# Attention plus int8 feed-forward on eight cores: value groups and projections in other slots, the last value product of the odd pairs one step earlier, one copy for a value group

## The chip, the cores and the metric

The kernel runs on all 8 NeuronCores of one Trainium2 chip, four cores to a die. Every core works on its own four sequences of the input and the cores exchange nothing. The metric is the device time of the slowest core in microseconds (us). Three runs of the kernel before gave 1652.48, 1654.83 and 1738.67 us, median 1654.83. The engines are called as in the profile: PE (matrix products), DVE (vector), ACT (scalar), POOL (GpSimd) and SP (the engine that issues most DMAs).

## The reference

The input is x, 32 sequences of 2048 rows of 1024 numbers. Rows are normalised, and two branches work on the result:

```python
xn = _layernorm(x, axis=-1)
x = x + _L0_attn_ref(xn, w_in, w_out) + _L0_ffn_ref(xn, weight_q, weight_scale, bias)
```

The attention has 16 heads of 64 and works in windows of 512 queries. Each window sees its own 512 keys and the 512 before it, of which the mask keeps those at a distance of 0 to 512; a bias that grows with the distance is added before the softmax. The first window of a sequence has no keys before it.

```python
scores = jnp.einsum('bhnqd,bhnkd->bhnqk', qb, k2) * scale
scores = jnp.where(valid, scores + bias, -jnp.inf)
p = jax.nn.softmax(scores, axis=-1)
out = jnp.einsum('bhnqk,bhnkd->bhnqd', p, v2)      # then times w_out
```

The feed-forward branch is a quantised linear layer: each row is scaled to at most 127 and rounded, multiplied by an int8 weight of 1024 by 1024, and scaled back.

## The kernel before, in words

A core holds 16 **blocks** of 512 rows, four to a sequence. The program is recorded by a Python loop (`for t ... for slot ... for i ...`, lines 856 to 957) which appends instructions to one list for each engine; every engine then executes its list strictly in that order and waits only on semaphores. A block has 8 **slots** (one for each pair of heads) and a slot has 5 **steps**. The text numbers the steps of a block from 0 to 39: step = 5 x slot + i.

In each step of a block the loop records these things, in this order.

- `scores` (slots 0 to 2) or `scores2` (slots 3 to 7) for one tile of 128 keys by 512 queries of a head pair. In slots 0 to 2 each step does its own. From slot 3 on, the even steps do the scores of two steps at once ("paired scores": steps 22 and 23 in step 22, steps 24 and 25 in step 24), into the two score buffers `sc0` and `sc1`, which alternate by step.
- `exps2` of an odd step in slots 3 to 7: ACT turns the scores into exponentials in `p`.
- the evacuations of the product group of the step before (list `after`), by ACT or DVE.
- `norm` if one is due: DVE multiplies the sums in `oa` and `ob` by the reciprocals and writes `ofm` (lines 845 and 848).
- `mask` of the step before: DVE multiplies `p` by a triangle (line 806).
- `den` if one is due: ACT makes the reciprocals of the row sums as Ln, Ln and Exp(-x) (lines 835, 837, 838). It waits for the last value product of its pair.
- `exps`, or `exps2` of an even step.
- one **dense group** from the table `PLAN`: 8 matmuls of 512 columns into one of two PSUM buffers `dn0`, `dn1`, used in turn. K and Q are the key and query projections, V the value projection of this block (`("V", half, chunk)`), F the int8 product and P the output projection of the block before (`("F", chunk, half)`). A `+` marks the next block. A third group can start only when the first one's buffer has been evacuated. V groups are evacuated by ACT (two copies, lines 627 and 628), F by DVE (line 649), P by DVE (line 681), after which POOL adds the residual (line 664) and SP stores the result; K and Q groups of pairs 3 to 7 by DVE (line 599), of pairs 0 to 2 by ACT and DVE.
- `pv`: the value products (line 822) of exponentials of earlier steps, by the table in braces at line 891: the tile of a slot's step i is multiplied at step i + 4, 4, 5, 5 and 6 counted from the tile's slot start for i = 0, 1, 2, 3, 4 (the first two 4 steps after the start, the next two 5, the last one 6).
- the preparation of the next block (statistics, normalisation) and of the rounded input of the block before (`xq_make`, three POOL operations for each half of a row tile; `xq_turn`, a DMA transpose on SP's queue), by tables of steps.

`den` stands 7 steps after its slot's start and `norm` one after it. For the pair of slot 3 (start 15) that is steps 22 and 23, for slot 4 (start 20) steps 27 and 28, for slot 5 (start 25) steps 32 and 33.

## Time and profile before

| what | value |
|---|---|
| runs | 1652.48, 1654.83, 1738.67 us |
| the profiled execution's own time | 1654.68 us |
| its span on the slowest core | 1653.1 us |
| spans of all cores | 1645.1 to 1653.1 us |
| granted clock, mean of each core | 0.992 to 0.994 |
| busy: PE, ACT, DVE, POOL | 95%, 64%, 57%, 51% |
| chain that ended last, by engine | PE 85%, ACT 6%, DMA 4% |

The profiled execution stands 0.15 us below the median of the runs. A matmul's row gives a start and a modelled duration; a matmul of 512 columns is listed with 0.38 us while the next one starts 0.22 us later, so the starts, not the durations, tell what PE spends. The time in square brackets behind a row is the idle time before it and what ended it.

### The profile page before, as it was taken

How to read it: one execution, taken by the hardware profiler on the slowest of the kernel's cores; microseconds unless marked ns; L12 is line 12 of the kernel's file. 1: busy time of each engine (PE TensorE's matmuls, PEld its weight loads, DVE VectorE, ACT ScalarE, POOL GpSimd, SP SyncE). 2: the span in 40 equal slices, each digit the busy share in tenths (PEclk: the TensorE clock that was granted, in tenths of full speed). 3: DMA queues.
4: the chain of work that ended last, by engine and by line, in shares of the span. 5: the costliest groups of instructions: out<-in, count | busy, mean ns of one | idle time of the engine just before them, and what ended most of it. 6: DMA issues, size and time to landing. Idle time of an engine off the chain costs nothing.

```text
span 1653.1 us, 29485 instructions; the slowest of 8 cores (1645.1 to 1653.1 us)
## 1 busy us (share of the span) xinstructions
PE 1566.1 (95%) x8568; PEld 749.9 (45%) x8736; DVE 939.6 (57%) x1696; ACT 1060.1 (64%) x2093; POOL 840.0 (51%) x1242
## 2 busy tenths in 40 slices
PE   4859999999999999999999999999999999999998
PEld 2325444454444445444444544445444444544443
DVE  4535646556475655746566564655647566564454
ACT  3546676766746667776665677667775566767662
POOL 5324536445473644536455563645537554563365
PEclk9979999999999999999999999999999999999999
DMA  7784453433545344353445434344354634435232
GB/s 161 185 222 116 124 147 107 128 116 122 147 133 151 115 128 121 113 146 114 128 132 149 142 109 136 113 121 135 109 141 127 173 116 115 141 109 147 78 79 82
DMA packets 208707, 213.98 MB, mean 129 GB/s; under 512 B 139932, under 2 KB 140060, under 8 KB 208040
## 3 DMA queue, kind: packets, MB, share of 16 engines
q1 hardware_dynamic: 205672, 201.60, 42.2%
q0 software_dynamic: 2880, 10.49, 3.5%
q8 instruction: 76, 1.25, 0.3%
q14 instruction: 79, 0.65, 0.2%
HBM read 149.12 MB, written 37.75 MB: 113 GB/s over the span
## 4 chain that ended last, share of the span: by engine, by line
PE 85%; ACT 6%; DMA 4%; issue 3%; DVE 1%; POOL 1%; SPq 0%; ACTq 0%; DVEq 0%; POOLq 0%
PE dn L578 61%; PE ob L822 7%; PE oa L822 7%; PE sc L730 5%; PE sc L753 5%; ACT p L770 4%; DMA wqk<-w 1%; DMA w2bf<-wqk 1%; ACT r L837 1%; ACT r L835 1%; DMA xpre<-x 1%; SPq L160 0%; DVE p L806 0%; POOL xn L462 0%; DMA xnfm<-xn 0%
## 5 line engine op out<-in xcount | busy, mean ns | idle before, releaser
L770 ACT ACTIVATE p<-sc,kbias_sb 128x512 bf16<-128x512 f32 (+3 forms) x1120 | 489.9, 536 | 235.8 <-PE sc L753 158.6
L578 PE MATMUL dn<-xnfm,wqk 128*128 128x512 bf16 x1996 | 477.1, 382 | 14.6 <-DMA xnfm<-xn 9.6
L664 POOL TENSOR_TENSOR u<-u,xres 128x256 f32<-128x256 f32 x240 | 169.9, 729 | 337.8 <-DVE u L681 337.5
L806 DVE TENSOR_TENSOR p<-p,tri_sb 128x512 bf16<-128x512 bf16 (+1 forms) x608 | 251.3, 414 | 146.4 <-ACT p L787 112.5
L578 PEld LDWEIGHTS dn<-xnfm,wqk 128*128 128x128 bf16 x2048 | 192.6, 98 | 244.5 <-issue 34.4
L787 ACT ACTIVATE p<-sc 128x1024 bf16<-128x1024 f32 (+3 forms) x228 | 214.9, 954 | 107.8 <-PE sc L730 105.9
L578 PE MATMUL dn<-wq_sb,xqfm 128*128 128x512 bf16 x1003 | 240.5, 381 | 6.0 <-DMA xqfm<-xq 2.8
L578 PE MATMUL dn<-wout_sb,ofm 128*128 128x512 bf16 x984 | 233.0, 379 | 6.5 <-issue 4.0
L578 PE MATMUL dn<-wv_sb,xnfm 128*128 128x512 bf16 x985 | 237.2, 380 | 2.0
L822 PE MATMUL oa<-p,vst 128*128 128x512 bf16 (+3 forms) x888 | 217.4, 300 | 4.6 <-DVE ofm L848 4.4
L822 PE MATMUL ob<-p,vst 128*128 128x256 bf16 (+3 forms) x896 | 218.7, 300 | 0.4
L649 DVE SCALAR_TENSOR_TENSOR u<-dn,small,wsb_sb 128x512 f32<-128x512 f32 x124 | 93.1, 751 | 166.9 <-PE dn L578 160.3
L681 DVE TENSOR_TENSOR u<-dn,u 128x512 f32<-128x512 f32 x124 | 85.8, 692 | 177.0 <-PE dn L578 165.3
L561 POOL TENSOR_TENSOR xres<-xres,biasb_sb 128x256 f32<-128x256 f32 x248 | 168.1, 709 | 0.0
L578 PEld LDWEIGHTS dn<-wv_sb,xnfm 128*128 128x128 bf16 x1024 | 97.6, 98 | 116.0 <-issue 10.7
L445 POOL TENSOR_SCALAR small<-small 128x1 f32<-128x1 f32 x64 | 12.3, 192 | 267.8 <-DVE small L444 267.8
L578 PEld LDWEIGHTS dn<-wq_sb,xqfm 128*128 128x128 bf16 x1024 | 96.6, 98 | 112.7 <-issue 13.8
L578 PEld LDWEIGHTS dn<-wout_sb,ofm 128*128 128x128 bf16 x1024 | 95.2, 98 | 114.2 <-issue 14.1
L753 PE MATMUL sc<-q,k 64*128 64x512 bf16 (+3 forms) x1120 | 117.4, 301 | 25.4 <-ACT p L770 22.4
L835 ACT ACTIVATE r<-oa 64x512 f32<-64x512 f32 x128 | 76.1, 594 | 87.8 <-PE ob L822 85.9
L822 PEld LDWEIGHTS oa<-p,vst 128*128 128x128 bf16 x896 | 87.9, 98 | 88.9 <-issue 8.3
L543 POOL TENSOR_SCALAR xqt<-xres,small 128x512 f32<-128x512 f32 x124 | 99.4, 802 | 40.3 <-DMA xres<-x 28.8
(61 smaller groups left out, 1634.4 us busy)
## 6 DMA issues: line engine op xcount, KB each, us to landing
wqk<-w2bf SPq DMA_DIRECT2D x240, 256.0 KB, 3.0
xpre<-x SPq DMA_DIRECT2D x64, 512.0 KB, 4.5
xres<-x SPq DMA_DIRECT2D x64, 512.0 KB, 4.5
out<-u SPq DMA_DIRECT2D x124, 256.0 KB, 2.2
wqk<-w POOLq DMA_DIRECT2D x16, 256.0 KB, 8.7
w2bf<-wqk SPq DMA_DIRECT2D x16, 256.0 KB, 5.5
wv_sb<-wv POOLq DMA_DIRECT2D x2, 1024.0 KB, 11.8
wq_sb<-wq POOLq DMA_DIRECT2D x1, 2048.0 KB, 13.8
```

The source lines that it names most:

```text
L543: a = P.op("gpsimd", lambda e, cols=cols: e.tensor_scalar(out=xqt[:, :], in0=buf[:, cols], scalar1=negm[g][:, tc:tc + 1], scalar2=alpha[g] ...
L561: xb_ready[(t, tc)] = P.op("gpsimd", lambda e, cols=cols: e.tensor_tensor(out=buf[:, cols], in0=buf[:, cols], in1=biasb_sb[:, cols], op=AL ...
L578: tok = P.op("tensor", lambda e, k=k: e.matmul(out=dn[b][:, :], lhsT=lhs(k), rhs=rhs(k), start=(k == 0), stop=(k == n - 1)), waits=(waits ...
L649: v = P.op("vector", lambda e: e.scalar_tensor_tensor(out=u[:, :], in0=dn[b][:, :], scalar=xs[g][:, tc:tc + 1], in1=wsb_sb[:, cols], op0=A ...
L664: a = P.op("gpsimd", lambda e, q=q: e.tensor_tensor(out=u[:, 256 * q:256 * q + 256], in0=u[:, 256 * q:256 * q + 256], in1=buf[:, 512 * hal ...
L681: v = P.op("vector", lambda e: e.tensor_tensor(out=u[:, :], in0=dn[b][:, :], in1=u[:, :], op=ALU.add), waits=[tok, u_ready[(t, tc, half)]])
L753: tok = P.op("tensor", lambda e, r=r, slot=slot, tc=tc, c0=c0, c1=c1, hp=hp: e.matmul(out=sc[b % 2][:, 512 * hp + c0:512 * hp + c1], lhsT= ...
L770: tok = P.op("scalar", lambda e, c0=c0, c1=c1, hp=hp, o=o: e.activation(out=pbuf[b % NPB][:, 512 * hp + c0:512 * hp + c1], in_=sc[b % 2][: ...
L787: exp_done[b] = P.op("scalar", lambda e: e.activation(out=pt, in_=st, func=AF.Exp, scale=SCALE), waits=[sc_done[b]] + p_free[b % NPB])
L806: mask_done[b] = P.op("vector", lambda e: e.tensor_tensor(out=pt, in0=pt, in1=m, op=ALU.mult), waits=[exp_done[b], c_tok])
L822: end=end: e.matmul(out=bank[:, c0:c1], lhsT=vlhs(h, slot, tc), rhs=pbuf[bp % NPB][:, 512 * hp + c0:512 * hp + c1], start=(j == TILES[0]), ...
L835: P.op("scalar", lambda e: e.activation(out=r[0:64, :], in_=oa[64:128, :], func=AF.Ln), waits=[tok] + r_free, inc=False)
```

## The change

Three things are changed, and the tables that depend on them.

1. The four V groups of the second half of the heads move from steps 5, 10, 15 and 20 to steps 5, 7, 10 and 12. The F and P groups that stood in between move back: in slots 3 and 4 the first three steps now hold F, P, F and P, F, P instead of V, F, P twice. The load, rounding and transpose of row tile 3 (`XR_LOAD`, `XQ_MAKE`, `XQ_TURN`) and the transpose of tile 2 move with them: the rounding of tile 3 from step 17 to step 22, its transpose from step 23 to 24, its load from step 15 to 18, the transpose of tile 2 from step 13 to 17.
2. For the pairs of slots 3, 5 and 7 the last value product comes 5 steps after the slot's start instead of 6, `den` 6 instead of 7, `norm` 7 instead of 8.
3. A V group is evacuated by one ACT copy of 128 partitions by 512 columns (a strided destination) instead of two of 256.

```diff
+PV_BEAT = {0: 4, 1: 4, 2: 5, 3: 5, 4: 6}
+PV_BEAT_ODD = {0: 4, 1: 4, 2: 5, 3: 5, 4: 5}
...
     [("V", 0, 1), ("V", 0, 2), ("V", 0, 3), ("K", 2, 0), ("Q", 2, 0)],
-    [("V", 1, 0), ("F", 0, 0), ("P", 0, 0), ("K", 3, 0), ("Q", 3, 0)],
-    [("V", 1, 1), ("F", 0, 1), ("P", 0, 1), ("K", 4, 0), ("Q", 4, 0)],
-    [("V", 1, 2), ("F", 1, 0), ("P", 1, 0), ("K", 5, 0), ("Q", 5, 0)],
-    [("V", 1, 3), ("F", 1, 1), ("P", 1, 1), ("K", 6, 0), ("Q", 6, 0)],
+    [("V", 1, 0), ("F", 0, 0), ("V", 1, 1), ("K", 3, 0), ("Q", 3, 0)],
+    [("V", 1, 2), ("P", 0, 0), ("V", 1, 3), ("K", 4, 0), ("Q", 4, 0)],
+    [("F", 0, 1), ("P", 0, 1), ("F", 1, 0), ("K", 5, 0), ("Q", 5, 0)],
+    [("P", 1, 0), ("F", 1, 1), ("P", 1, 1), ("K", 6, 0), ("Q", 6, 0)],
...
-XR_LOAD = {(3, 0): 3}
-XQ_MAKE = {(0, 2): 1, (1, 3): 2, (3, 2): 3}
+XR_LOAD = {(3, 3): 3}
+XQ_MAKE = {(0, 2): 1, (1, 3): 2, (4, 2): 3}
...
-XQ_TURN = {(0, 4): 1, (2, 3): 2, (4, 3): 3}
+XQ_TURN = {(0, 4): 1, (3, 2): 2, (4, 4): 3}
...
         def vdst(slot, tc, half):
             o = ((slot * 4 + tc) * 8 + half * 4) * 192
-            v = vst[:, o:o + 768].rearrange("p (a c) -> p a c", a=4)
-            first = v[:, :, 0:64]
-            second = v[:, :, 128:192]
-            return first, second
+            v = vst[:, o:o + 768].rearrange("p (a h d) -> p a h d", a=4, h=3)
+            return v[:, :, 0:3:2, :]
...
-                s = P.op("scalar", lambda e: e.copy(out=first, in_=src[:, :, 0, :]), waits=[tok] + old)
-                s2 = P.op("scalar", lambda e: e.copy(out=second, in_=src[:, :, 1, :]))
+                s2 = P.op("scalar", lambda e: e.copy(
+                    out=vdst(t % 2, tc, half), in_=dn[b][:, :].rearrange("p (a h d) -> p a h d", a=4, h=2)),
+                    waits=[tok] + old)
...
-                            beat = b - i + {0: 4, 1: 4, 2: 5, 3: 5, 4: 6}[i]
+                            beat = b - i + (PV_BEAT_ODD if halves and slot % 2 else PV_BEAT)[i]
...
-                            den_plan[base + 7] = (tp, pp, tok)
+                            den_plan[base + (6 if pp >= PAIR2 and pp % 2 else 7)] = (tp, pp, tok)
```

How the rows stand on PE around step 20, in the second block of a sequence. The first fence is the kernel before, from step 20's group to the paired scores of step 22: `p4` is the last tile of slot 3, `sc0` and `sc1` are the scores.

```order
L578 MATMUL dn1<-wv_sb,xnfm 128x512 x8
L822 MATMUL oa<-p2,vst 128x256 x2
L822 MATMUL ob<-p2,vst 128x256 x2
L822 MATMUL oa<-p3,vst 128x384
L822 MATMUL oa<-p3,vst 128x128
L822 MATMUL ob<-p3,vst 128x384
L822 MATMUL ob<-p3,vst 128x128
L578 MATMUL dn0<-wq_sb,xqfm1 128x512 x8
L822 MATMUL oa<-p4,vst 128x512
L822 MATMUL ob<-p4,vst 128x512
L753 MATMUL sc0<-q2,k2 128x256 x4
L753 MATMUL sc1<-q2,k2 128x384 x2
```

And the changed kernel, the same stretch.

```order
L580 MATMUL dn1<-wout_sb,ofm0 128x512 x8
L823 MATMUL oa<-p2,vst 128x256 x2
L823 MATMUL ob<-p2,vst 128x256 x2
L823 MATMUL oa<-p3,vst 128x384
L823 MATMUL oa<-p3,vst 128x128
L823 MATMUL ob<-p3,vst 128x384
L823 MATMUL ob<-p3,vst 128x128
L823 MATMUL oa<-p4,vst 128x512
L823 MATMUL ob<-p4,vst 128x512
L580 MATMUL dn0<-wq_sb,xqfm1 128x512 x8
L754 MATMUL sc0<-q2,k2 128x256 x4
L754 MATMUL sc1<-q2,k2 128x384 x2
```

The products of `p4` stand ahead of the group of step 21 instead of behind it, and the V group of step 20 is a P group.

On ACT, from the exponentials of step 20 to those of step 22, before:

```order
L770 ACTIVATE p0<-sc0,kbias_sb 128x512 x2
L770 ACTIVATE p1<-sc1,kbias_sb 128x128 x2
L770 ACTIVATE p1<-sc1,kbias_sb 128x384 x2
L627 CAST vst<-dn1 128x4x64
L628 CAST vst<-dn1 128x4x64
L835 ACTIVATE r<-oa 64x512
L837 ACTIVATE r<-ob 64x512
L838 ACTIVATE r<-r 128x512
L770 ACTIVATE p2<-sc0,kbias_sb 128x256 x4
```

and changed:

```order
L771 ACTIVATE p0<-sc0,kbias_sb 128x512 x2
L771 ACTIVATE p1<-sc1,kbias_sb 128x128 x2
L771 ACTIVATE p1<-sc1,kbias_sb 128x384 x2
L836 ACTIVATE r<-oa 64x512
L838 ACTIVATE r<-ob 64x512
L839 ACTIVATE r<-r 128x512
L771 ACTIVATE p2<-sc0,kbias_sb 128x256 x4
```

The three reciprocal instructions stand at the same place, behind the exponentials of step 21 and ahead of those of step 22; the two copies of the V group are gone from here.

On DVE, from the mask of step 19 (`p4`) to the evacuation of the K group of step 23, before:

```order
L806 TENSOR_TENSOR p4<-p4,tri_sb 128x2x128
L806 TENSOR_TENSOR p0<-p0,tri_sb 128x2x128
L441 BN_STATS small<-xpre1 128x6
L443 BN_STATS small<-xpre1 128x6
L444 BN_AGGR small<-small 128x2
L649 SCALAR_TENSOR_TENSOR u3<-dn0,small,wsb_sb 128x512
L806 TENSOR_TENSOR p1<-p1,tri_sb 128x2x256
L681 TENSOR_TENSOR u3<-dn1,u3 128x512
L845 TENSOR_TENSOR ofm1<-oa,r 64x512
L848 TENSOR_TENSOR ofm1<-ob,r 64x512
L806 TENSOR_TENSOR p2<-p2,tri_sb 128x2x256
L599 CAST k2<-dn0 128x512
```

and changed:

```order
L807 TENSOR_TENSOR p4<-p4,tri_sb 128x2x128
L682 TENSOR_TENSOR u2<-dn1,u2 128x512
L807 TENSOR_TENSOR p0<-p0,tri_sb 128x2x128
L443 BN_STATS small<-xpre1 128x6
L445 BN_STATS small<-xpre1 128x6
L446 BN_AGGR small<-small 128x2
L650 SCALAR_TENSOR_TENSOR u3<-dn0,small,wsb_sb 128x512
L846 TENSOR_TENSOR ofm1<-oa,r 64x512
L849 TENSOR_TENSOR ofm1<-ob,r 64x512
L807 TENSOR_TENSOR p1<-p1,tri_sb 128x2x256
L682 TENSOR_TENSOR u3<-dn1,u3 128x512
L807 TENSOR_TENSOR p2<-p2,tri_sb 128x2x256
L601 CAST k2<-dn0 128x512
```

DVE has one more group to evacuate here (line 682 for `u2`, the P group of step 20), and the two `ofm` operations stand ahead of the mask of `p1` and the evacuation of `u3` by line 682 instead of behind them.

## Rows read from the trace of the kernel before

**Rows 1.** The page: the span, and the busy time of each engine.

```profile
span 1653.1 us, 29485 instructions; the slowest of 8 cores (1645.1 to 1653.1 us)
...
PE 1566.1 (95%) x8568; PEld 749.9 (45%) x8736; DVE 939.6 (57%) x1696; ACT 1060.1 (64%) x2093; POOL 840.0 (51%) x1242
```

**Rows 2.** PE's waits over the span: waited for, us in total, times, longest.

```profile
PE sc L753 <- ACT p L770: 22.4, 30, 1.6
...
PE dn L578 <- DMA xnfm<-xn: 9.6, 1, 9.6
...
PE dn L578 <- DVE u L649: 1.7, 11, 0.2
```

**Rows 3.** Timeline of PE, three of 24 waits: start, us, what, [idle before].

```profile
190.33 0.39 PE L753 MATMUL sc<-q,k 64*128 64x512 bf16 x2 [0.71 <-ACT p L770]
...
585.64 0.39 PE L753 MATMUL sc<-q,k 64*128 64x512 bf16 x2 [0.71 <-ACT p L770]
...
1607.98 0.39 PE L753 MATMUL sc<-q,k 64*128 64x512 bf16 x2 [0.71 <-ACT p L770]
```

**Rows 4.** Timeline of PE, steps 20 to 25 of a block in mid-sequence.

```profile
677.97 0.61 PE L753 MATMUL sc<-q,k 64*128 64x512 bf16 x6
...
681.12 1.89 PE L578 MATMUL dn<-wq_sb,xqfm 128*128 128x512 bf16 x8
682.85 0.38 PE L822 MATMUL oa<-p,vst 128*128 128x512 bf16 x1
683.06 0.38 PE L822 MATMUL ob<-p,vst 128*128 128x512 bf16 x1
683.37 0.61 PE L753 MATMUL sc<-q,k 64*128 64x256 bf16 x8
...
687.48 0.39 PE L753 MATMUL sc<-q,k 64*128 64x512 bf16 x2
688.57 0.39 PE L753 MATMUL sc<-q,k 64*128 64x512 bf16 x2 [0.71 <-ACT p L770]
```

**Rows 5.** Timeline of ACT over the same steps.

```profile
678.46 2.73 ACT L770 ACTIVATE p<-sc,kbias_sb 128x512 bf16<-128x512 f32 x6 [1.91 <-PE sc L753]
...
683.59 0.59 ACT L835 ACTIVATE r<-oa 64x512 f32<-64x512 f32 x1 [1.87 <-PE ob L822]
...
685.42 4.17 ACT L770 ACTIVATE p<-sc,kbias_sb 128x256 bf16<-128x256 f32 x10
```

**Rows 6.** ACT by form: count, busy us, mean ns, idle before.

```profile
L628 ACT CAST vst<-dn 128x256 bf16<-128x256 f32 x128 | 49.4, 386 | 0.0
...
L611 ACT CAST qa<-dn 64x512 bf16<-64x512 f32 x48 | 28.0, 583 | 15.4 <-PE dn L578 14.9
```

**Rows 7.** Timeline of DVE and POOL over the same steps, and POOL's next wait.

```profile
683.85 0.41 DVE L806 TENSOR_TENSOR p<-p,tri_sb 128x512 bf16<-128x512 bf16 x1
...
684.42 1.12 POOL L462 TENSOR_SCALAR xn<-xpre,small 128x1024 bf16<-128x1024 f32 x1 [0.18 <-POOL small L455]
...
688.19 4.23 POOL L561 TENSOR_TENSOR xres<-xres,biasb_sb 128x256 f32<-128x256 f32 x6
...
689.16 0.80 DVE L806 TENSOR_TENSOR p<-p,tri_sb 128x512 bf16<-128x512 bf16 x1
...
699.87 1.41 POOL L664 TENSOR_TENSOR u<-u,xres 128x256 f32<-128x256 f32 x2 [6.20 <-DVE u L681]
```

**Rows 8.** The page: evacuation of a P group on DVE, first rounding operation on POOL.

```profile
L681 DVE TENSOR_TENSOR u<-dn,u 128x512 f32<-128x512 f32 x124 | 85.8, 692 | 177.0 <-PE dn L578 165.3
...
L543 POOL TENSOR_SCALAR xqt<-xres,small 128x512 f32<-128x512 f32 x124 | 99.4, 802 | 40.3 <-DMA xres<-x 28.8
```

**Rows 9.** The chain that ended last, in the first block.

```profile
79.76 9.31 DMA wqk<-w
...
89.12 18.19 DMA w2bf<-wqk
```

**Rows 10.** Timeline of PE in the last 25 us.

```profile
1635.83 13.97 PE L578 MATMUL dn<-wout_sb,ofm 128*128 128x512 bf16 x63 [0.58 <-DVE ofm L848]
```

More of the change, by code:

```diff
@@ L623, in evac @@
             def evac():
-                first, second = vdst(t % 2, tc, half)
-                src = dn[b][:, :].rearrange("p (a h d) -> p a h d", a=4, h=2)
                 old = v_seen.get((t % 2, half), [])
-                s = P.op("scalar", lambda e: e.copy(out=first, in_=src[:, :, 0, :]), waits=[tok] + old)
-                s2 = P.op("scalar", lambda e: e.copy(out=second, in_=src[:, :, 1, :]))
+                s2 = P.op("scalar", lambda e: e.copy(
+                    out=vdst(t % 2, tc, half), in_=dn[b][:, :].rearrange("p (a h d) -> p a h d", a=4, h=2)),
+                    waits=[tok] + old)
                 dn_free[b] = [s2]
```

## The prediction, made before the run

> **What bounds the kernel now.** I first read the page. The span is 1653.1 us, PE is busy for 95% of it and the next engine, ACT, for 64% [rows 1]. A kernel like this becomes faster only where PE waits. So the second view is the list of PE's waits [rows 2]. The largest entry is the paired scores (line 753) waiting for the exponentials (line 770): 22.4 us in 30 places. The next, 9.6 us once, is the transposed input of the second block, a start-up matter. Third, the timeline of PE through the whole span: 24 of those 30 waits have the same 0.71 us and come at two places of every block that is not the first of its sequence (12 such blocks); the first, the last and one in the middle are shown [rows 3]; the other 6 lie in the first 102 us. The two places are steps 24 and 34, where the scores of two steps (24 and 25, 34 and 35) are written together.
>
> The fourth view is one such place in full, on PE [rows 4] and on ACT [rows 5]. The reader is to see this chain. The last value product of the pair of slot 3 starts at 683.06, behind the group of step 21 that starts at 681.12. The reciprocals wait for it and start at 683.59. They hold ACT until the next exponentials start at 685.42, which is 1.83 us. The scores for these exponentials had started at 683.37; undisturbed, exponentials start 0.49 us behind the start of their scores (677.97 to 678.46), so they could have started at 683.86 and came 1.56 us late. The exponentials of steps 22 and 23 follow one another on ACT, the second score buffer comes free late, and the scores of step 25 start at 688.57.
>
> **What such a wait costs.** A pair of score matmuls of 512 columns has started at 687.48. Two value products of 512 columns start 0.21 us apart (682.85, 683.06) [rows 4]. So the scores of step 25 could have started at 687.69 and started 0.88 us later. The listed idle time is 0.71 us, because the row's duration of 0.39 us overlaps the next start. The two are the ends of the price: 24 x 0.71 = 17.0 us and 24 x 0.88 = 21.1 us. I take 21.1, because it is made of starts, which move the end, and the 0.71 starts from a modelled end.
>
> **Part 1: value product, reciprocals and norm one step earlier.** Nothing is added or removed. On ACT the order does not change: the reciprocals stand behind the exponentials of step 21 and ahead of those of step 22, as before. What changes is what they wait for. The last value product now stands ahead of the group of step 21, so its first matmul starts where that group started, 681.12, and its second at 681.33. The reciprocals start 0.53 us behind that (683.06 to 683.59), at 681.86, and end the block at 683.69. The scores of step 22 still start at 683.37, since PE has the same work ahead of them, and land for ACT at 683.86. So the reciprocals fit into ACT's gap with 0.17 us to spare, the exponentials start 1.56 us earlier, and the score buffer is free at 688.57 - 1.56 = 687.01 where PE wants it at 687.69. The wait goes, with 0.68 us of slack. Step 34 has the same order. Gain: 24 x 0.88 = **21.1 us**.
>
> The wait that the change adds: the value product now waits for the mask of step 19 one group earlier. Behind it on PE would stand everything. But the scores of step 21 already needed the exponentials of step 19 (same buffer), and one group of 8 matmuls and the products of two tiles lie between, so I cost it at nothing. In slot 7 the reciprocals move ahead of the exponentials of the next block's step 1. PE has no listed wait there; ACT is late by up to their 1.83 us, behind which wait an evacuation and the scores two steps on, with a group of step length in between. Nothing, with 1.8 us as the upper end of a delay that only one of 15 places would have to show.
>
> At the very end, the first output projection waits 0.58 us for the norm of the last pair [rows 10], which stood behind the evacuation of an F group and now stands ahead of it. Gain: **0.6 us**.
>
> **Part 2: groups in other slots.** PE's work is the same. Slots 3 and 4 lose one ACT evacuation each and gain one on DVE of about 0.69 us (line 681) [rows 8]. In slots 1 and 2 it is the other way, and ACT has room there, since its exponentials there cause PE no wait after the start. The tightest place on DVE is step 22: behind the reciprocals (683.69 by part 1) come at most one evacuation and the two norm operations, about 0.7 us each, to 685.8. The P group of step 22, evacuated next, starts 0.54 us behind the scores at 683.37 (eight matmuls of 256 columns, two side by side, at 0.21 us for 512 columns, and a little for the change of tile shape) and takes 1.73 us as its neighbour does (681.12 to 682.85) [rows 4], to 685.6. Its buffer is wanted again two groups on, at 687.69 plus a pair. So DVE is on time. The rounding of tile 3 moves on POOL from step 17 to step 22, behind the normalisation at 684.42 [rows 7]: six operations, each at most the 0.80 us of the first kind [rows 8], 4.8 us. POOL next has a residual, the biases that started at 688.19 (eight in a row, 5.5 us by the six shown in 4.23) and then waits 6.20 us for DVE until 699.87 [rows 7]. The 4.8 us and a residual of 1.4 us, that of the P group which comes from step 17 to step 20, fill that gap to the brim: 6.2 us, while part of the residual and of the rounding falls where POOL waited earlier, before 684. SP's queue holds the store of step 22's P group in front of weight loads; it can be 4.8 us later. The loads are for groups two slots on, and the transposes of the next block's input stand 6 steps on. Cost: 0, cover: POOL's 6.2 us gap; if it is used up, the next thing late is the store of step 27's P group and those transposes.
>
> **Part 3: one copy for a V group.** 128 copies fewer. The pair took 2 x 0.39 us, overlapped. For one copy of 128 by 512 the nearest rows are the copy of 64 partitions by 512 columns, 583 ns, and the old half, 386 ns [rows 6]; I take 0.58, since columns set the time. ACT is saved up to 0.2 us each, none of it in front of a PE wait that is still there. Gain 0, at most a few tenths.
>
> **Start.** In the first block there are no F and P groups, so slots 1 and 2 hold one V group more each and slots 3 and 4 none. The chain there goes through DMAs: 9.31 us for weights that are issued when a Q group of slot 3 ends, then 18.19 us [rows 9]. That Q group has one more V group ahead of it (1.73 us [rows 4], 1.8 with its gaps) minus what PE waited there for ACT and the input. I take 0, between -1 and +1.8.
>
> **Sum.** 1654.68 - 21.1 - 0.6 = **1633.0 us**. The profiled execution is within 0.2 us of the median of the runs, 1654.83, so no correction is made. That is 1.3% less, inside the 2% about which a measurement of this kernel can tell from no change.
>
> **Rivals.**
> - *The wait comes back in slots 3 and 4 in another name.* Step 24's gain needs DVE to evacuate three groups in a row on time; step 34's place has no new work. For it: DVE has the F and P groups, the norm and the statistics within three steps, and in the first block of a sequence a step is shorter. Against: PE's waits for a group's evacuation on DVE are 1.7 us in 11 places now [rows 2]. Then half is gained: 1654.7 - 10.6 - 0.6 = 1643.5 us.
> - *The change does not do what it says.* ACT's order is unchanged, and the start of the exponentials is 683.86 against reciprocals that end at 683.69. If the value product waits for its mask, or something else holds ACT, both waits stay: 1654 us.
> - *DVE becomes the bound in slots 3 and 4, and the kernel is slower.* The mask of 128 x 512 took 0.41 us at 683.85 and 0.80 us at 689.16, when POOL added biases [rows 7]. If the moved POOL work stretches the ten masks of slots 3 and 4 by that 0.39 us, DVE has 3.9 us more per block. Should half of it reach PE, 15 blocks x 1.95 = 29 us, and the time is 1633 + 29 = 1662 us. It is slower than before from 1.45 us a block on. Against it: the moved operations are tensor-scalar operations on POOL, not the additions beside which the long mask stood.
> - *The start goes well too, or PE's spacing hides more.* 1627 us.
>
> The Trainium skill, page "Advanced Engine Details and Errata", section "Miscellaneous Facts", GPSIMD Details, says that POOL shares a read and a write interface with DVE and conflicts with DVE instructions that have two SBUF inputs, as the mask has. By that rule the third rival's stretch is to be expected whatever POOL runs, and its 1662 us would be the forecast; the trace's 0.41 and 0.80 us agree that there is a conflict, but not that it reaches PE.
>
> **Chances and range.** Forecast with both waits gone and no new one, 1630 to 1636: 0.60. Half gained, 1637 to 1649: 0.20. No effect, 1650 to 1657: 0.09. Slower by the DVE: 0.07. Below 1630: 0.04. The range takes in the forecast, its lower price end (1654.7 - 17.0 = 1637.7) and the half case with the start's bounds: 1629 to 1648. More than 2% faster would need a time below 1621.7, which is half as much again as all the waits of this kind: 0.02. More than 2% slower, above 1687.9, needs the third rival with nothing hidden (15 x 3.9 = 58 us, 1691): 0.03. Within 2%: 0.95.
>
> **What would show it.** In the changed kernel's list of PE's waits, the scores of line 753 waiting for the exponentials should fall from 30 places to 6 or fewer, and from 22.4 us to about 5. The distance from a block's step 24 to the next block's, 102.93 us now (585.64 to 688.57) [rows 3, 4], should be 1.76 us less, 101.2 us. In ACT's timeline the reciprocals of slots 3 and 5 should end about 0.2 us ahead of the next exponentials. The V copies should be listed near 0.58 us. The prediction is wrong if PE shows new waits for DVE at lines 649, 681 or 845 to 848 in slots 3 and 4, if the input transposes wait for SP, or if the 0.71 us stand again at steps 24 and 34.

## The result and the profile after

The changed kernel took 1635.34 us (median; runs 1635.67, 1635.0, 1634.25 and 1636.84), against 1654.83 before. The ratio is 0.9882, with a 95% interval of [0.9861, 0.9904]: 1.2% faster, and clearly so. Two repeats beside other kernels gave 0.9892 [0.9878, 0.9907] and 0.9883 [0.9866, 0.9899]. Executions in which the cores of one die show a lower granted clock and take longer (1826.42 us beside 1633.81 in one of the kernels below) are left out of every ratio.

The page of the changed kernel: the span, the busy time of each engine, and further down the shares of the chain that ended last.

```profile
span 1634.0 us, 29478 instructions; the slowest of 8 cores (1624.4 to 1634.0 us)
...
PE 1577.8 (97%) x8736; PEld 748.2 (46%) x8736; DVE 937.4 (57%) x1696; ACT 1056.2 (65%) x1965; POOL 834.9 (51%) x1242
...
PE 93%; DMA 4%; POOL 1%; issue 1%; ACT 1%; DVE 0%; SPq 0%; POOLq 0%; DVEq 0%; ACTq 0%
```

Against [rows 1] PE went from 95% to 97%, and DVE, ACT and POOL kept their work. A part of PE's rise is in the record only: the trace of the kernel before lacks 168 of the 8736 matmuls. ACT left the chain almost wholly (6% before).

PE's waits over the whole span, changed kernel: waited for, us in total, times, longest.

```profile
PE dn L503 <- POOL small L447: 16.6, 2, 13.2
PE oa L823 <- DVE ofm L849: 12.6, 3, 8.4
PE sc L754 <- ACT p L771: 6.7, 8, 1.2
...
PE dn L580 <- DMA xqfm<-xq: 2.8, 1, 2.8
PE dn L580 <- DVE u L650: 1.9, 1, 1.9
PE dn L580 <- DMA xnfm<-xn: 1.8, 1, 1.8
```

The entry that led [rows 2] with 22.4 us in 30 places is 6.7 us in 8, all before 111 us. The same list for the stretch from 120 to 1580 us names 15.6 us in 22 places before and nothing after. The 1.9 us is new; it is in the last block and is taken up below. The 9.6 us for `xnfm` is now 1.8, and the wait of `oa` for `ofm` is 12.6 us where it was 4.4; that is no gain and no loss but one start-up delay under another name: the second block's first K group starts at 116.35 before and at 118.19 here.

PE at steps 20 to 25, to be laid beside [rows 4]: start, duration, line, what.

```profile
675.79 0.38 PE L823 MATMUL oa<-p,vst 128*128 128x512 bf16 x1
676.00 0.38 PE L823 MATMUL ob<-p,vst 128*128 128x512 bf16 x1
676.22 1.89 PE L580 MATMUL dn<-wq_sb,xqfm 128*128 128x512 bf16 x8
678.04 0.61 PE L754 MATMUL sc<-q,k 64*128 64x256 bf16 x8
678.59 1.90 PE L580 MATMUL dn<-wout_sb,ofm 128*128 128x512 bf16 x8
680.32 1.89 PE L580 MATMUL dn<-xnfm,wqk 128*128 128x512 bf16 x8
682.14 0.61 PE L754 MATMUL sc<-q,k 64*128 64x512 bf16 x4
```

ACT in the same steps, to be laid beside [rows 5].

```profile
676.53 0.59 ACT L836 ACTIVATE r<-oa 64x512 f32<-64x512 f32 x1 [0.68 <-PE ob L823]
677.14 0.59 ACT L838 ACTIVATE r<-ob 64x512 f32<-64x512 f32 x1
677.82 0.63 ACT L839 ACTIVATE r<-r 128x512 f32<-128x512 f32 x1
678.54 3.03 ACT L771 ACTIVATE p<-sc,kbias_sb 128x256 bf16<-128x256 f32 x8
682.64 1.27 ACT L771 ACTIVATE p<-sc,kbias_sb 128x512 bf16<-128x512 f32 x2 [1.07 <-PE sc L754]
```

The reciprocals start at 676.53, 0.53 us behind the last value product's second matmul at 676.00, and would be through after 1.83 us at 678.36. The scores start at 678.04 and the exponentials 0.50 us later, which is the undisturbed distance of 0.49. The scores of steps 24 and 25 stand in one row of four at 682.14, without a wait in between. Step 30's scores start at 596.32 in one block and at 697.48 in the next: 101.16 us, where the kernel before had 102.93 between its steps 24.

**Where the time went, core by core.** The cores reach the second block at quite different times, in any of the kernels: before, between 108.4 and 116.4 us. So the kernels are compared below by the *rest*: a core's span less the start of its second block (its first K group), as a mean over the eight cores (seven where one core's record lacks that row). It is 1536.45 us before and 1515.50 after, in the repeats 1516.30 and 1515.57: 20.2 to 21.0 us less. On the two slowest cores (2 before, 3 after) the profiled executions differ as follows.

| stretch | before | after | difference |
|---|---|---|---|
| to the second block | 116.35 | 118.19 | +1.84 |
| from there to the K group of step 28 in the last block | 1476.60 | 1456.04 | -20.56 |
| from there to the first F group of the last tile (tile 3 of the last block) | 37.02 | 37.20 | +0.18 |
| from there to the first closing output projection | 5.86 | 4.93 | -0.93 |
| from there to the end | 17.27 | 17.64 | +0.37 |
| sum | 1653.1 | 1634.0 | -19.1 |

### The profile page after: what moved, and what is told of

The parts are those of the page before. It is cut to its first block, busy times and chain, and to the rows that moved or that the text cites. A ratio compares the mean times of both kernels' runs of the same rounds, so it can differ in the third digit from the quotient of the medians.

```text
span 1634.0 us, 29478 instructions; the slowest of 8 cores (1624.4 to 1634.0 us)
## 1 busy us (share of the span) xinstructions
PE 1577.8 (97%) x8736; PEld 748.2 (46%) x8736; DVE 937.4 (57%) x1696; ACT 1056.2 (65%) x1965; POOL 834.9 (51%) x1242
## 4 chain that ended last, share of the span: by engine, by line
PE 93%; DMA 4%; POOL 1%; issue 1%; ACT 1%; DVE 0%; SPq 0%; POOLq 0%; DVEq 0%; ACTq 0%
PE dn L580 67%; PE oa L823 7%; PE ob L823 7%; PE sc L754 6%; PE sc L731 5%; DMA wqk<-w 1%; DMA w2bf<-wqk 1%; DMA xpre<-x 1%; SPq L164 0%; ACT p L771 0%; DMA xqfm<-xq 0%; DMA xnfm<-xn 0%; POOL xn L464 0%; POOL xres L563 0%; POOL small L457 0%
## 5 line engine op out<-in xcount | busy, mean ns | idle before, releaser
L580 PE MATMUL dn<-xnfm,wqk 128*128 128x512 bf16 x2048 | 482.1, 382 | 3.5 <-DMA xnfm<-xn 1.8
L580 PE MATMUL dn<-wv_sb,xnfm 128*128 128x512 bf16 x1024 | 242.9, 380 | 0.0
L580 PE MATMUL dn<-wout_sb,ofm 128*128 128x512 bf16 x1024 | 241.7, 380 | 0.0
L823 PE MATMUL oa<-p,vst 128*128 128x256 bf16 (+3 forms) x896 | 220.9, 301 | 12.7 <-DVE ofm L849 12.6
L580 PEld LDWEIGHTS dn<-wq_sb,xqfm 128*128 128x128 bf16 x1024 | 97.6, 98 | 120.2 <-issue 14.7
L846 DVE TENSOR_TENSOR ofm<-oa,r 64x512 bf16<-64x512 f32 x128 | 87.0, 680 | 106.7 <-ACT r L839 104.7
L580 PEld LDWEIGHTS dn<-wout_sb,ofm 128*128 128x128 bf16 x1024 | 92.8, 98 | 119.7 <-issue 22.4
L754 PE MATMUL sc<-q,k 64*128 64x512 bf16 (+3 forms) x1120 | 113.5, 301 | 9.8 <-ACT p L771 6.7
L552 POOL TENSOR_SCALAR xq<-xqt 128x512 bf16<-128x512 f32 x128 | 79.4, 620 | 81.4 <-DMA xqfm<-xq 60.3
```

The costliest lines, as they stand in the source:

```text
L580: tok = P.op("tensor", lambda e, k=k: e.matmul(out=dn[b][:, :], lhsT=lhs(k), rhs=rhs(k), start=(k == 0), stop=(k == n - 1)), waits=(waits ...
L754: tok = P.op("tensor", lambda e, r=r, slot=slot, tc=tc, c0=c0, c1=c1, hp=hp: e.matmul(out=sc[b % 2][:, 512 * hp + c0:512 * hp + c1], lhsT= ...
L823: end=end: e.matmul(out=bank[:, c0:c1], lhsT=vlhs(h, slot, tc), rhs=pbuf[bp % NPB][:, 512 * hp + c0:512 * hp + c1], start=(j == TILES[0]), ...
L846: P.op("vector", lambda e: e.tensor_tensor(out=dst[0:64, 512 * p:512 * (p + 1)], in0=oa[0:64, :], in1=r[0:64, :], op=ALU.mult), waits=[tok ...
```

## The experiments

The theory: the whole gain is that the last value product of slots 3, 5 and 7 stands one step earlier, at 0.88 us for each of 24 waits, and the groups' new slots and the single copy are worth nothing. Its rivals: that the groups' slots pay for a part, or cost something that hides a larger gain; that the start moved; and, for the 2 us by which the forecast was too low, that something was given back in the last block.

| kernel | ratio to before, 95% interval | rest, us | waits of the scores for ACT between 120 and 1580 us | PE's waits for `xnfm` between 125 and 1570 us, mean of the cores |
|---|---|---|---|---|
| before | 1 | 1536.45 | 15.6 us, 22 | none |
| after | 0.9882 [0.9861, 0.9904] | 1515.50 | none | 0.41 us |
| value product, reciprocals and norm alone | 0.9877 [0.9861, 0.9893] | 1515.09 | none | none |
| groups' slots alone | 1.0006 [0.9995, 1.0017] | 1536.32 | 15.6 us, 22 | none |
| one copy alone | 1.0006 [0.9987, 1.0026] | 1535.46 | 15.6 us, 22 | none |
| pair of slot 3 alone | 0.9949 [0.9937, 0.9962] | 1526.29 | 7.8 us, 11 | none |
| value product moved, reciprocals and norm not | 0.9890 [0.9874, 0.9906] | 1516.56 | none | none |
| first block by the old table | 0.9883 [0.9869, 0.9897] | 1516.90 | none | 1.36 us |
| last block: F and P groups reordered | 0.9911 [0.9897, 0.9925] | 1521.19 | none | 0.90 us |
| last block: one F group earlier | 0.9869 [0.9854, 0.9883] | 1514.29 | none | 0.45 us |
| the first part alone and one F group earlier | 0.9858 [0.9843, 0.9873] | 1513.42 | none | none |

**The first part alone.** The kernel before with the value products' table and the steps of `den` and `norm` of the changed one:

```diff
-                            beat = b - i + {0: 4, 1: 4, 2: 5, 3: 5, 4: 6}[i]
+                            beat = b - i + (PV_BEAT_ODD if halves and slot % 2 else PV_BEAT)[i]
-                            den_plan[base + 7] = (tp, pp, tok)
+                            den_plan[base + (6 if pp >= PAIR2 and pp % 2 else 7)] = (tp, pp, tok)
```

> Only the last value product, the reciprocals and the norm of the pairs of slots 3, 5 and 7 are one step earlier; groups and copies as before. Theory (the wait of 0.88 us at steps 24 and 34 hangs on the start of that value product): all 24 waits go but the last, which is given back in the last block, so about 20 us less than before, 1634 to 1636 us, and the start is as before. Rival (the V copies on ACT or the groups' new places are part of the cure): at step 24 the wait stays, at step 34 it goes, 10 to 11 us less, about 1644 us.

Median 1633.02 us, ratio 0.9877 [0.9861, 0.9893]: the whole gain. It was repeated beside the changed kernel.

> Only the earlier value product, reciprocals and norm, once more, on the same chip as the changed kernel. Theory (the new places of the groups and the one copy are worth nothing): the same as the changed kernel within 0.1%, 1633 to 1636 us. Rival (the groups' new places cost a little): 2 to 3 us faster than the changed kernel, as the first run of it suggests.

> The changed kernel itself, beside the others: 1634 to 1637 us.

1633.66 against 1635.97 us, 0.9876 [0.9858, 0.9894] against 0.9883 [0.9866, 0.9899]. The rest was 1514.43 against 1515.57. The intervals overlap. The medians differ by 2.3 us in both pairs, the rests by 0.4 and 1.1 us. The difference in the rests is the price of the groups' new slots, which the paragraph on the first block of a sequence shows.

**The groups' slots alone.** The changed kernel with the value product, the reciprocals, the norm and the two copies as before; the table `PLAN` and the tables of row tile 3 are the new ones.

> Only the groups are in their new slots, with the tables of loads, rounding and transposes that go with them; value products and copies as before. Theory: the waits of 0.71 us stand at steps 24 and 34 as before, since the reciprocals still wait for the value product behind the group of step 21; the first block is 1 to 2 us longer; 1655 to 1657 us. Rival (freeing ACT of the V copies in slots 3 and 4 is worth something): the 12 waits at step 24 shrink, up to 10 us less, 1645 us. Rival (DVE becomes late): above 1660 us.

1.0006 [0.9995, 1.0017]. The waits stay, as PE's list of this kernel says:

```profile
PE sc L753 <- ACT p L770: 23.7, 33, 1.2
```

So taking ACT's V copies out of slots 3 and 4 removes no wait, although a pair of them stood right ahead of the reciprocals: ACT had been waiting for the value product there, not working.

**One copy alone.** The kernel before with the single copy of 128 by 512.

> Only the V group's evacuation is one copy. Theory: the copy takes 0.58 us for two that took 0.65 us together, nothing waits for it; no change, within 1 us of before. Rival: ACT at step 24 starts its next work earlier; it cannot, since it is idle for 1.87 us there waiting for the value product.

1.0006 [0.9987, 1.0026]. ACT by form, this kernel: count, busy us, mean ns, idle before.

```profile
L623 ACT CAST vst<-dn 128x512 bf16<-128x512 f32 x128 | 75.6, 590 | 61.1 <-PE dn L576 61.1
```

The two copies took 377 and 386 ns, 128 times, 97.6 us if added up; but the second started about 0.27 us behind the first, so that the pair kept ACT busy for 0.65 us, 83.3 us in all. One copy takes 75.6. ACT's busy time fell by 7 us, from 1060.1 to 1052.9 us, and what was saved went into its idle time.

**The value product without the reciprocals.** The changed kernel with one line of the kernel before:

```diff
-                            den_plan[base + (6 if pp >= PAIR2 and pp % 2 else 7)] = (tp, pp, tok)
+                            den_plan[base + 7] = (tp, pp, tok)
```

> The changed kernel, but only the last value product of slots 3, 5 and 7 is early: the reciprocals and the norm are recorded 7 and 8 steps behind the slot's start, as before. Theory: the reciprocals stand at the same place in ACT's list either way (behind the exponentials of the odd step, ahead of the even step's), so the time is that of the changed kernel, plus the 0.6 us at the end where the first output projection waits for the norm: 1635 to 1636.5 us. Rival (the step in which the reciprocals are recorded is what counts): the 0.71 us waits come back, 1654 us.

> The changed kernel itself, as the measure for the runs beside it: 1634 to 1637 us.

0.9890 [0.9874, 0.9906] against 0.9892 [0.9878, 0.9907] of the changed kernel in a repeat. Where the reciprocals are recorded brings none of the waits at steps 24 and 34 back; what they wait for decides. What came back is the wait of the closing output projection for the norm [rows 10], on PE's timeline of this kernel:

```profile
1614.58 10.73 PE L580 MATMUL dn<-wout_sb,ofm 128*128 128x512 bf16 x49 [0.57 <-DVE ofm L849]
```

In the last block PE also waits longer at step 39 than in the changed kernel, 2.82 us instead of 1.87, and 1.11 instead of 2.80 at the next wait behind it.

**Half of the waits.** The first part alone, and of it only the pair of slot 3 (12 of the 24 places):

```diff
-                            beat = b - i + (PV_BEAT_ODD if halves and slot % 2 else PV_BEAT)[i]
+                            beat = b - i + (PV_BEAT_ODD if halves and slot == 3 else PV_BEAT)[i]
-                            den_plan[base + (6 if pp >= PAIR2 and pp % 2 else 7)] = (tp, pp, tok)
+                            den_plan[base + (6 if pp == 3 else 7)] = (tp, pp, tok)
```

> The kernel before with the value product, reciprocals and norm of the pair of slot 3 alone one step earlier. Theory: the 12 waits at step 24 go and the 12 at step 34 stay; 12 x 0.88 = 10.6 us less than before, 1644 us. By the listed idle time of 0.71 us each it would be 8.5 us, 1646 us.

0.9949 [0.9937, 0.9962], and the rest fell by 10.16 us, 0.85 us for each of the 12 (10.66 us, 0.89 for each, if only the stretch up to step 28 of the last block is taken). That is the price by starts (12 x 0.88 = 10.6) rather than by listed idle time (12 x 0.71 = 8.5). Over PE's whole list the scores wait in 17 places here:

```profile
PE sc L755 <- ACT p L772: 13.9, 17, 1.6
```

**The first block.** The changed kernel with the groups of the first block in their old slots (`PLAN_FIRST` is the old table):

```diff
-                        dense(t, LAST_SLOT[i] if t == NT - 1 and slot == 7 else PLAN[slot][i])
+                        dense(t, LAST_SLOT[i] if t == NT - 1 and slot == 7 else (PLAN_FIRST if t == 0 else PLAN)[slot][i])
```

> The changed kernel with the value groups of the very first block in their old slots. Theory (the second block's start is set by the weight and transpose DMAs and scatters from core to core by 8 us, whatever the groups do): no change against the changed kernel, within 1 us. Rival (the value group that stands ahead of the last Q group delays the DMA chain): 1 to 2 us faster than the changed kernel, with the mean start of the second block over the cores at 112 us instead of 114.

0.9883 [0.9869, 0.9897]. The second block starts at 112.0 us in the mean of the cores, against 113.9, 112.2 and 112.7 in three profiles of the changed kernel and 112.1 before. The start is worth nothing that can be seen beside this scatter.

**The first block of a sequence.** In the first block of the second, third and fourth sequence the steps are shorter, since its windows have fewer keys, and there the groups' new slots do cost something. The rows are POOL's residual ahead of a store, the four transposes of the next block's input on SP's queue behind that store, and the K group that reads them. The kernel before, core 0:

```profile
891.12 1.41 POOL L664 TENSOR_TENSOR u<-u,xres 128x256 f32<-128x256 f32 x2 [3.75 <-DVE u L681]
894.22 5.57 SPq L160 DMA_TRANSPOSE xnfm<-xn  x4
905.48 1.89 PE L578 MATMUL dn<-xnfm,wqk 128*128 128x512 bf16 x8
```

A repeat of the changed kernel, core 0:

```profile
880.68 1.46 POOL L665 TENSOR_TENSOR u<-u,xres 128x256 f32<-128x256 f32 x2
883.56 6.63 SPq L164 DMA_TRANSPOSE xnfm<-xn  x4
894.35 1.89 PE L580 MATMUL dn<-xnfm,wqk 128*128 128x512 bf16 x8 [1.40 <-DMA xnfm<-xn]
```

Before, POOL waited 3.75 us for DVE ahead of this residual. With the rounding of tile 3 moved ahead of it POOL comes without a wait, and later: the transposes start 9.4 us ahead of the point where PE wants the input, instead of 11.3. In three profiles of the changed kernel PE waits here in 4, 8 and 7 of 24 places (three blocks, eight cores), for 0.5 to 1.6 us each, which is 0.41, 0.96 and 0.80 us for a core in the mean; in the two profiles of the first part alone it waits in none. The stretch from the second block to step 28 of the last is 1456.49, 1457.16 and 1456.60 us in the mean of the cores with the new slots, 1456.26 and 1455.80 without; less these waits all five lie between 1455.8 and 1456.3. The kernel with the groups' slots alone and the one with the reciprocals left behind have the same short distance (9.2 us in the mean) and no such wait; why not is open. A second price stands at the very end: from the start of the last matmul to the end it is 3.71 us on nearly every core before and 4.09 on every core of the changed kernel, and from the first closing projection on 17.69 us in the mean of the cores with the new slots, those alone included, against 17.3 to 17.4 without. Its cause was not looked for. Both together are 1 us: 1515.8 us is the mean rest of the three profiles, 1514.8 that of the two without the new slots.

**The last block.** First the place, on PE in the changed kernel: the K group of step 28, the group of step 39 (`FO`, tile 2 of the last block's own rounded rows) and the first group of tile 3.

```profile
1574.23 3.63 PE L580 MATMUL dn<-xnfm,wqk 128*128 128x512 bf16 x16
...
1602.85 1.89 PE L580 MATMUL dn<-wq_sb,xqfm 128*128 128x512 bf16 x8 [1.87 <-DVE u L650]
...
1611.43 5.09 PE L580 MATMUL dn<-wq_sb,xqfm 128*128 128x512 bf16 x16 [2.80 <-DMA xqfm<-xq]
```

The same three in the kernel before:

```profile
1592.95 3.63 PE L578 MATMUL dn<-xnfm,wqk 128*128 128x512 bf16 x16
...
1621.33 1.89 PE L578 MATMUL dn<-wq_sb,xqfm 128*128 128x512 bf16 x8 [0.75 <-DVE p L806]
...
1629.97 2.29 PE L578 MATMUL dn<-wq_sb,xqfm 128*128 128x512 bf16 x5 [2.85 <-DMA xqfm<-xq]
```

Step 34 with its wait of 0.88 us lies between them [rows 3, the third], and yet the stretch from the first to the last is 37.02 us before and 37.20 after, where 36.14 was to be expected. The waits in it are 3.60 us before and 4.67 after: 1.07 us more. What PE waits for at step 39 is named by DVE's last semaphore, but DVE had long been done; what ended last there is a transpose. SP's queue, changed kernel:

```profile
1590.99 1.33 SPq L164 DMA_TRANSPOSE xqfm<-xq  x1
...
1599.04 0.33 SPq L158 DMA_DIRECT2D out<-u  x1
1599.46 1.31 SPq L164 DMA_TRANSPOSE xqfm<-xq  x1
```

And POOL:

```profile
1557.32 1.41 POOL L665 TENSOR_TENSOR u<-u,xres 128x256 f32<-128x256 f32 x2 [8.11 <-DVE p L807]
...
1588.91 1.59 POOL L665 TENSOR_TENSOR u<-u,xres 128x256 f32<-128x256 f32 x2
...
1594.31 0.62 POOL L552 TENSOR_SCALAR xq<-xqt 128x512 bf16<-128x512 f32 x1 [2.17 <-DMA xqfm<-xq]
...
1597.38 1.58 POOL L665 TENSOR_TENSOR u<-u,xres 128x256 f32<-128x256 f32 x2
```

Read backwards: the transpose of tile 2 (1599.46) stands behind a store, this behind a residual (1597.38), this behind the rounding of tile 2, of which one operation waited 2.17 us for the transpose of tile 1 (1590.99). That one stands behind the store of the residual that ends at 1590.50, and from 1557.32 up to there POOL waits for no other engine: 33 us of its own work in a row. In the kernel before POOL had still waited for DVE ahead of that residual, but only for 0.61 us:

```profile
1606.24 1.41 POOL L664 TENSOR_TENSOR u<-u,xres 128x256 f32<-128x256 f32 x2 [0.61 <-DVE u L681]
```

So in the last block, where POOL rounds the block's own rows as well, it was within 0.6 us of setting the pace. PE became 0.88 us faster at step 24 and again at step 34, and POOL and the transposes did not follow. The experiments move the transpose of tile 1 ahead of that store. The first brings both F groups of tile 3 and the roundings forward and mixes `FO` and P groups:

```diff
-LAST_SLOT = [("FO", 0, 0), ("FO", 0, 1), ("FO", 1, 0), ("FO", 1, 1), ("FO", 2, 0)]
+LAST_SLOTS = {6: [("F", 3, 0), ("F", 3, 1), ("P", 2, 1), ("FO", 0, 0), ("FO", 0, 1)],
+              7: [("P", 3, 0), ("P", 3, 1), ("FO", 1, 0), ("FO", 1, 1), ("FO", 2, 0)]}
-LAST_MAKE = {(4, 4): 0, (5, 3): 1, (6, 4): 2, (7, 2): 3}
-LAST_TURN = {(5, 2): 0, (6, 3): 1, (7, 2): 2, (7, 4): 3}
+LAST_MAKE = {(4, 4): 0, (5, 3): 1, (6, 3): 2, (7, 1): 3}
+LAST_TURN = {(5, 2): 0, (6, 2): 1, (7, 0): 2, (7, 4): 3}
```

> The changed kernel with the groups of the last two slots of the last block in another order: both F groups of row tile 3 and the two groups of the last block's first row tile come two steps earlier, the P groups two later, and the rounding and transposes with them. Theory (in slot 7 of the last block PE waits for a chain of transpose, rounding and store that hangs on the F group of step 33, so the 0.88 us gained at step 34 were given back): the wait of 1.9 us in slot 7 and the one of 2.8 us behind it go, 4 to 5 us less than the changed kernel, about 1631 us. Rival (the wait of 1.9 us is DVE being late behind the norm and stretched masks): the 1.9 us stay, only the 2.8 us go.

It failed: 0.9911 [0.9897, 0.9925], the rest 5.7 us longer than the changed kernel's. PE and DVE, this kernel:

```profile
1606.97 3.57 PE L581 MATMUL dn<-wq_sb,xqfm 128*128 128x512 bf16 x8 [6.36 <-DVE u L651]
```

```profile
1606.08 0.75 DVE L651 SCALAR_TENSOR_TENSOR u<-dn,small,wsb_sb 128x512 f32<-128x512 f32 x1 [6.17 <-DMA out<-u]
```

With the `FO` groups ahead of the last P groups, an `FO` evacuation wanted a `u` buffer whose content was not yet stored; DVE waited 6.17 us for the store and PE 6.36 us behind it. The second experiment moves one F group and keeps the order of users of `u`:

```diff
-LAST_SLOT = [("FO", 0, 0), ("FO", 0, 1), ("FO", 1, 0), ("FO", 1, 1), ("FO", 2, 0)]
+LAST_SLOTS = {6: [("F", 3, 0), ("F", 3, 1), ("P", 2, 1), ("P", 3, 0), ("P", 3, 1)],
+              7: [("FO", 0, 0), ("FO", 0, 1), ("FO", 1, 0), ("FO", 1, 1), ("FO", 2, 0)]}
-LAST_MAKE = {(4, 4): 0, (5, 3): 1, (6, 4): 2, (7, 2): 3}
-LAST_TURN = {(5, 2): 0, (6, 3): 1, (7, 2): 2, (7, 4): 3}
+LAST_MAKE = {(4, 4): 0, (5, 3): 1, (6, 3): 2, (7, 2): 3}
+LAST_TURN = {(5, 2): 0, (6, 2): 1, (7, 2): 2, (7, 4): 3}
```

> The changed kernel; in slot 6 of the last block only, the two F groups of row tile 3 come first (steps 30 and 31 instead of 31 and 33) and the transpose and rounding behind them one step earlier. Theory (the wait of 1.9 us in slot 7 of the last block is the chain of transpose, rounding and store that hangs on the second F group): that wait goes and the 2.8 us wait behind it stays; 1.9 us less than the changed kernel, 0.1%, to be seen in the trace as the time from the second block's start to the end, 1516 to 1514 us. Rival (DVE is late behind the norm and the masks): the wait stays.

0.9869 [0.9854, 0.9883] beside 0.9883 [0.9866, 0.9899] for the changed kernel; the rest is 1.2 to 2.0 us shorter. PE's wait in slot 7 shrinks from 1.87 us:

```profile
1599.60 1.89 PE L581 MATMUL dn<-wq_sb,xqfm 128*128 128x512 bf16 x8 [0.22 <-DVE ofm L850]
```

The transpose of tile 2 is issued at 1596.22 there, 23.59 us after step 28's group, instead of 25.23. The time as such is shorter by the rest and by the stretches below; the two ratios' intervals overlap.

**Both together.** The first part alone with this last block.

> The kernel before with the earlier value product, reciprocals and norm, the old places of the groups, two copies, and the last block's F groups early as in the run beside it. Theory: the wait of 2.5 us that stands in slot 7 without it goes; 1631 to 1633 us, the fastest of all.

Median 1632.05 us, 0.9858 [0.9843, 0.9873], the rest 1513.42: the shortest of all by both measures, without the groups' new slots and without the single copy. On PE the two last groups of slot 7 run through as one row, and the wait for the transposes of tile 3 stays:

```profile
1595.15 3.89 PE L581 MATMUL dn<-wq_sb,xqfm 128*128 128x512 bf16 x16
...
1605.92 5.30 PE L581 MATMUL dn<-wq_sb,xqfm 128*128 128x512 bf16 x16 [2.98 <-DMA xqfm<-xq]
```

It beats the kernel before clearly, and the changed one beside it (1635.97 us) by 3.9 us in the medians with intervals that just overlap; its lead over the changed kernel with one F group earlier is within the noise.

The end of all these kernels by starts on PE, of the slowest core of each:

| kernel | step 28 to tile 3's first group, us | from there to the first closing projection | sum | sum, mean of the eight cores |
|---|---|---|---|---|
| before | 37.02 | 5.86 | 42.88 | 42.59 |
| after | 37.20 | 4.93 | 42.13 | 41.32 |
| value product moved, reciprocals not | 38.14 | 4.19 | 42.33 | 42.69 |
| the first part alone | 37.78 | 3.45 | 41.23 | 41.49 |
| one F group earlier | 35.72 | 5.14 | 40.86 | 40.14 |
| the first part and one F group earlier | 35.62 | 5.14 | 40.76 | 40.12 |

With both the step-34 wait and the norm's 0.58 us gained the sum on the slowest core would be 41.42. The first part alone seems to reach it there, with more given back in its first stretch and a short second one. But the second stretch is 3.45 or about 5 us long on different cores of one and the same profile, by the clock (see the last section), and in the mean of the cores the first part alone and the changed kernel do not differ. The first stretch hardly scatters: 36.96 to 37.02 us on the cores before, 37.16 to 37.21 after, so that the step-34 wait is given back on all of them. One F group earlier is worth 1.2 us in the mean.

## Why the prediction held, and where it did not

The mechanism and its price were right. The step that failed is the one from the size to what a measurement can tell, and the term of the sum that was mis-sized is the 24th wait; a term that was put at nothing, the groups' new slots, costs about 1 us.

- **What the measurement can tell: wrong, and the most serious mistake.** The forecast of 1.3% was the right size, but the text put it "inside the 2% about which a measurement of this kernel can tell from no change", and gave 0.02 to a gain of more than 2%, 0.95 to a time within it. The runs showed 0.9882 with an interval of 0.2% to either side, and the runs quoted for before already agreed within 0.15% but for one. A clear gain was forecast and called no change.
- **Which waits go: right.** 24 of 30 were to go and the list to fall to about 5 us in 6 places; it is 6.7 in 8, none of them in mid-kernel. The first part alone gives all of it.
- **The price by starts: right.** Up to step 28 of the last block 23 waits were removed, 20.2 us by 0.88 and 16.3 by 0.71; the stretch is 20.56 us shorter. The distance from block to block is 101.16 us where 101.2 was forecast, and twelve waits gave 0.85 us each.
- **The reciprocals fit into ACT's gap with 0.17 us to spare: right.** They end about 0.18 us ahead of the exponentials.
- **The norm at the end, 0.6 us: right.** That wait is gone in the changed kernel and stands at 0.57 us again where the norm alone was left behind.
- **The 24th wait: wrong.** The sum counted 24 x 0.88 and looked only at the neighbourhood of steps 24 and 34. In the last block the wait at step 34 lay beside POOL's chain of residuals, stores, roundings and transposes, for which PE waits at step 39 and at tile 3; these two waits grew together by 1.07 us. With it the sum is 1633.0 + 1.1 = 1634.1; the profiled execution has 1635.67. Of the other terms, on the slowest core, the later start is 1.84 us, which no part of the change explains, and the end behind the first closing projection 0.37; the clock at tile 3 and the stretch before step 28 give 0.7 back.
- **Groups in other slots, 0: wrong by about 1 us.** The cover was read in a block of mid-sequence, and there it held. POOL ran the moved rounding from 681.77 to 686.91, 5.1 us where 4.8 were costed, and still waited 5.87 us for DVE ahead of 700.94. DVE evacuated the P group of step 22 at 680.82 and PE had no wait for it. In the first block of a sequence POOL's wait had been 3.75 us and not 6.20, and it was used up; the next thing late was what the prediction had named, the transposes of the next block's input, and one of its signs of being wrong is there, on some cores. The slowest core of the profile of the changed kernel had no such wait.
- **One copy, 0.58 us each, worth nothing: right** (585 ns). ACT is saved 0.06 us for each, not up to 0.2.
- **Start, 0 between -1 and +1.8: right**, with a scatter from core to core that is wider than the bounds.
- **The rival "half gained" did not occur**, nor did the one on DVE, but the argument against the latter was weak. It said that masks are stretched by POOL's additions and the moved operations are tensor-scalar ones. In the changed kernel a mask of 128 by 512 took 0.81 us beside such a rounding operation, and 0.42 us at another place:

```profile
680.36 0.42 DVE L807 TENSOR_TENSOR p<-p,tri_sb 128x512 bf16<-128x512 bf16 x1
...
682.93 0.81 DVE L807 TENSOR_TENSOR p<-p,tri_sb 128x512 bf16<-128x512 bf16 x1
```

```profile
682.85 0.62 POOL L549 TENSOR_SCALAR xqt<-xqt 128x512 f32<-128x512 f32 x1 [0.16 <-POOL xqt L545]
```

  The mean of these masks was 489 ns before, 468 with the first part alone, 535 with the groups' slots alone. So the stretch is real and does not depend on POOL adding. It did not reach PE, whose list names no wait for DVE between 120 and 1580 us. The Trainium skill, in "Advanced Engine Details and Errata", section "Miscellaneous Facts", under GPSIMD Details, says that POOL shares a read and a write interface with DVE and conflicts with DVE instructions that have two SBUF inputs, and makes no difference between POOL's operations. These rows agree with it.

## What to carry to other kernels

Price a wait by the distance of starts against an undisturbed neighbour of the same kind, and for every wait that is removed ask whether another engine works through without a wait beside it and is waited for behind it: there the wait is given back. Read the room that moved work needs in the tightest block, not in the usual one. Where the releaser comes late because of its place in its own engine's order, move it there; taking work off the engine that waits for it gained nothing here. Before a gain is called too small to see, look at how closely the runs agree. And compare stretches over all cores, since the slowest one alone also brings its own start and its own clock.

## What the runs showed of the hardware

A wait of PE can cost more than itself, when the clock falls behind it. The windows of the changed kernel's slowest core around the last transposes: us, busy time and count of PE, PEld, DVE, ACT and POOL, then the granted clock, DMA share and GB/s.

```profile
1608.50:1611.40 2.90, 0.13 (x1) 0.00 (x0) 0.60 (x1) 1.81 (x3) 2.90 (x5) 0.94 0.46 90
1611.40:1614.00 2.60, 2.57 (x7) 0.95 (x8) 0.78 (x2) 0.00 (x0) 2.60 (x5) 0.50 0.00 0
```

After 2.80 us of idle time PE ran at 0.50, its lower level of 1.2 GHz, for more than 2.6 us. The 16 matmuls from 1611.43 to the output projections at 1616.36 took 4.93 us, against 16 x 0.216 = 3.46 at full clock: the wait of 2.80 us cost 4.3. But the same wait does not always have this effect. Core 5 of the same execution, its timeline and its clock in the same place:

```profile
1608.04 3.61 PE L580 MATMUL dn<-wq_sb,xqfm 128*128 128x512 bf16 x16 [2.76 <-DMA xqfm<-xq]
...
1608.00:1610.60 2.60, 2.56 (x12) 1.20 (x13) 1.40 (x3) 0.00 (x0) 2.60 (x5) 1.00 0.00 0
```

The clock stayed at 1.00, and the output projections started at 1611.49, 3.45 us later. The wait was 2.76 to 2.81 us on all eight cores; on four of them the 16 matmuls took 3.45 us, on the other four 4.74 to 4.93. In the kernel before all eight cores fell, with one copy alone four. What decides between the two is not shown. Behind the 6.36 us of the failed last block and behind 2.49 us in the first part alone the next group of eight took 3.57 and 3.06 us; behind 1.87, 1.07 and 0.71 us the groups ran on at 0.216 us a matmul. In the first part alone PE of the slowest core fell back behind step 39's wait of 2.49 us, where it only shortened the next wait to 1.07 us, and ran tile 3's 16 matmuls at full clock in 3.45 us:

```profile
1602.07 3.06 PE L580 MATMUL dn<-wq_sb,xqfm 128*128 128x512 bf16 x8 [2.49 <-DVE p L808]
...
1610.61 3.61 PE L580 MATMUL dn<-wq_sb,xqfm 128*128 128x512 bf16 x16 [1.07 <-DMA xqfm<-xq]
```

The wait for tile 3's transposes, 2.98 us in the best kernel and on five of its cores 1.7 more by the clock (5.14 us for the 16 matmuls), is the next thing to go for. Whether it can be removed was not tried.
